# Second half of the row scores issued between the two subtractions on TensorE

## The chip, the cores and the metric

The kernel runs on one core of one Trainium2 chip. The metric is the device time of one execution in microseconds, lower is better. The core has five engines with a program each: TensorE (PE; its weight loads are shown as PEld), VectorE (DVE), ScalarE (ACT), GpSimd (POOL) and SyncE (SP, which here only issues DMAs). They meet through semaphores.

## The reference

32 sequences of 128 tokens, width 128, go through four blocks. In short, with 16 heads of 8:

```
x = block0(x):  x += g * attn(adaLN(x), mask_qk);  x += g * attn(adaLN(x), ctx, mask_kv);  x += g * gelu-MLP(adaLN(x))
x = block1(x):  x += gate * out(mixture of 3 experts over [LN(x), evidence(ctx), anchor])
x = block2(x):  x += attn(adaLN(x), adaLN(ctx))
x = block3(x):  x += attn(adaLN(x));  x += attn(x, ctx);  x += gelu-MLP(adaLN(x))

attn: s = q @ k.T / sqrt(8);  s = where(mask, s, lowest);  a = softmax(s);  out = a @ v
```

Five of these layers are attentions: two over 128 keys (the first of them masked over query and key, with rotary embedding), three over the 77 context tokens (the first masked over keys).

## The kernel before, in words

**Jobs.** An attention layer has 32 jobs, one per sequence; four jobs make a quad, and projections and norms are done per quad. Layers 0 and 1 (jobs 0 to 63) form phase 0, layers 2 to 4 (jobs 64 to 159) phase 1; between the phases stand the first MLP and the mixture of experts, after phase 1 the last MLP. In the text the layers are: masked (128 keys, `l0`), context with key mask (`l0c`, 77 keys), context (`l2`, 77), plain (`l3s`, 128) and last context (`l3c`, 77).

**Two sets of scores.** Each job's scores are made twice. *Row scores* (`rows`, line 645, made in reduced precision into `row_scores`, queries on partitions) serve only to find the maximum of each row; VectorE reads them (`row_max`, line 1215, tile `negmax`). They come in two halves of eight heads, h=0 and h=1, and both halves use the same two PSUM banks: a half can be written only when the maximum of the half before has been taken (the wait on `max_done` in `rows` and, for the masked layer, in `mask_rows`). *Exact scores* (`exact`, line 687, 16 products with keys on partitions into four banks of `scores`) feed the softmax. The row maximum is subtracted on TensorE by a product for each half (`shift`, line 707); then ScalarE takes the exponential of that half (`exponentiate`, line 1723, tile `p`), and `weigh` (line 720) multiplies with the values into `weighed`. `turn_blocks` on VectorE (line 1231, `nat`) takes that out.

**Masks.** In the masked layer mask products of 8 small matmuls each are added: `mask_rows` (closing for h=0, opening for h=1) and `mask_scores` (opening half 0 before the exact scores, closing half 1 after its subtraction).

**The order.** Each engine runs its own loop over slots t; the order inside a slot is written by hand. On TensorE (`attention`, line 757) slot t issued: the opening mask and the row scores of job t+5, half 1; exact scores and both subtractions of job t; `weigh` of job t-1; row scores of job t+6, half 0; then `quad_work`, which is in each quad of four slots a K projection, a transposition (norm or x), a value and output projection, and a Q projection (lines 793 to 817). `exact(t)` waits until both exponentials of job t-1 are done and for the DMAs of the pair (`stack_pair`, line 2116, SP's queue); `scores_read` holds it until a bank of `scores` that `quad_work` used has been read. On VectorE (line 1364) slot t runs: maximum of job t+5 half 1, reciprocal and transposition of older jobs, maximum of job t+6 half 0, norm statistics, rotations, residuals and `turn_blocks` of job t-1. GpSimd spreads the keys for the row scores (`spread_k`, line 1915, tile `kblk_r`), and waits for both halves of job t+5 before it writes those of job t+7.

The names used below: R0 and R1 are the row scores of half 0 and 1 (line 663), E the exact scores (line 700), S0 and S1 the subtractions (line 715), W is `weigh` (line 730).

Of the kernel before, what the change touches and what calls it, by code (L numbers as in the profile page):

```python
# [90 lines left out]
def layer_of(q):  # L91
    return LAYERS[q // NB]
# [92 lines left out]
def build(nc, a, out_x):  # L185
    with ExitStack() as ctx:
# [221 lines left out]
        def folding_at(t, hi):  # L408

            return t - 4 * hi - 5 if 0 <= t - 4 * hi - 5 < FOLDING else None  # L410
# [46 lines left out]
        def turned_in_quads(it):  # L457


            return not it.family or 0 < 4 * PHASES[it.q >= 2 * NB][1] - it.slot <= 5  # L460
# [25 lines left out]
        def row_banks(n, h):  # L486
            return scores[:, 2:4, :] if h == 0 and first_quad(n) else row_scores[:, :, :]

        def row_banks_read(n, h):
            return max_done, 2 * n + h - (1 if first_quad(n) else 0)  # L490
# [44 lines left out]
        def tensor_program(e):  # L535
# [93 lines left out]
            def mask_rows(n, h, opens):  # L629

                if layer_of(n // QUAD).mask == "qk":
                    w.wait_ge(dve_setup, DVE_AT["neg_qk"])
                    w.wait_ge(act_setup, ACT_AT["ident_bf"])
                    if opens:
                        w.wait_ge(*row_banks_read(n, h))
                    for i in range(2):
                        at = slice(TILE * (2 * h + i), TILE * (2 * h + i + 1))
                        for c in range(NG):
                            mm = e.matmul(row_banks(n, h)[TILE * c:TILE * (c + 1), i, :], ident_bf[at, at],
                                          neg_qk[at, c, :].unsqueeze(1).to_broadcast([TILE, NJ, S]), start=opens,  # L640
                                          stop=not opens, skip_group_check=True, tile_position=(TILE * (2 * h + i), TILE * c))
                    if not opens:
                        mm.then_inc(rows_done, 1)
# [113 lines left out]
            def attention(phase, first=-16, last=None):  # L757

                lo, hi = PHASES[phase]
                end = 4 * hi + TAIL if last is None else 4 * lo + last  # L760
                jobs, quads, norm_at = range(4 * lo, 4 * hi), range(lo, hi), NORM_AT[phase]

                def scores_read(t):

                    qi, cl = divmod(t, QUAD)
                    if t in norm_at and not turned_in_quads(norm_at[t]):
                        w.wait_ge(*turned_read(norm_at[t]))
                    if cl == 2 and qi - 2 in quads and qi >= hi:
                        w.wait_ge(wo_read, qi - 1)
                    if cl == 2 and qi + 1 in quads:  # L770
                        w.wait_ge(v_done, qi + 2)

                def quads_read(t):

                    qi, cl = divmod(t, QUAD)
                    if cl == 0 and qi + 2 in quads and qi + 2 != 0:
                        if layer_of(qi + 2).rope:
                            w.wait_ge(rope_half, 4 * (qi + 2) + 4)
                        else:
                            w.wait_ge(k_done, qi + 2 - NB + 1)  # L780
                    if cl == 1 and qi + 3 in quads and layer_of(qi + 3).name == "l3c":
                        w.wait_ge(raw_done, (qi + 3) % NB + 1)
                    if t in norm_at and turned_in_quads(norm_at[t]):
                        w.wait_ge(*turned_read(norm_at[t]))
                    if cl == 2 and qi - 2 in quads and qi < hi:
                        w.wait_ge(wo_read, qi - 1)
                    if cl == 3 and qi + 3 in quads:
                        if layer_of(qi + 3).rope:
                            w.wait_ge(rope_half, 4 * (qi + 3) + 2)
                        else:  # L790
                            w.wait_ge(q_done, qi + 3 - NB + 1)

                def quad_work(t, qi, cl):
                    early = max(min(2 * t + 1, 8 * hi), 8 * lo)
                    if cl == 2 and qi + 1 in quads:
                        w.wait_ge(exp_done, early)
                        project_v(qi + 1)
                    if t in norm_at and not turned_in_quads(norm_at[t]):
                        w.wait_ge(exp_done, early)
                        turn_normed(norm_at[t])  # L800
                    if t == -2 * QUAD:
                        project_k(0)
                    if cl in (0, 3) or t in norm_at or cl == 1 and qi + 3 in quads or cl == 2 and qi - 2 in quads:
                        for back in range(1, QUAD + 1):
                            quads_read(t - back)
                    if cl == 0 and qi + 2 in quads and t != -2 * QUAD:
                        project_k(qi + 2)
                    if cl == 1 and qi + 3 in quads and layer_of(qi + 3).name == "l3c":
                        turn_x(qi + 3)
                    if t in norm_at and turned_in_quads(norm_at[t]):  # L810
                        turn_normed(norm_at[t])
                    if cl == 2 and qi - 2 in quads:
                        if qi >= hi:
                            w.wait_ge(exp_done, early)
                        project_out(qi - 2)
                    if cl == 3 and qi + 3 in quads:
                        project_q(qi + 3)

                for t in range(4 * lo + first, end):
                    qi, cl = divmod(t, QUAD)  # L820
                    masked = t in jobs and layer_of(qi).mask == "qk"
                    if t + 5 in jobs:
                        mask_rows(t + 5, 1, True)
                    if t in (4 * lo, 4 * lo + 1):
                        w.wait_ge(max_done, 8 * lo + 8)
                    if masked:
                        scores_read(t - 1)
                        mask_scores(t, 0)
                    if t + 5 in jobs:
                        rows(t + 5, 1)  # L830
                    scores_read(t - 1)
                    if t in jobs:
                        exact(t)
                        shift(t, 0)
                        shift(t, 1)
                    if masked:
                        mask_scores(t, 1)
                        if cl == 3 and qi + 1 in quads:
                            w.wait_ge(nblk_done, qi + 2)
                    if phase == 1 and t in (4 * lo - 2, 4 * lo - 1):  # L840
                        keep_busy(4, av_bank[:, 0:128])
                    if t == 4 * hi:
                        first_layer(phase, 0, hi, range(2))
                    if t - 1 in jobs:
                        weigh(t - 1)
                    if t + 6 in jobs:
                        rows(t + 6, 0)
                        mask_rows(t + 6, 0, False)
                    if t in (-6, -4, -3):
                        keep_busy(3, scores[:, 0, 0:128])  # L850
                    if not masked and cl == 3 and qi + 1 in quads:
                        turn_max(qi + 1)
                    quad_work(t, qi, cl)
                    if masked and cl == 2 and qi + 1 in quads:
                        turn_max(qi + 1)
                    if phase == 0 and last is None:
                        first_prototypes(t - 4 * hi)
                    if t == -11:
                        modulate(range(2, 9))
                    if t == -8:  # L860
                        gates_and_context()
                    if t == -7:
                        w.wait_ge(act_setup, ACT_AT["l0mod1"])
                        keep_busy(5, scores[:, 0, 0:128])
                    c = first_layer_at(t, hi)
                    if c is not None:
                        first_layer(phase, c, hi, range(0 if c else 2, 4))
                    if second_layer_at(t, hi) is not None:
                        second_layer(phase, second_layer_at(t, hi), hi)
                    if phase == 0 and folding_at(t, hi) is not None:  # L870
                        fold_weights(folding_at(t, hi))
# [1414 lines left out]
```

## Time and profile before

| | us |
|---|---|
| three runs | 1036.22, 1025.52, 1047.08 (median 1036.22) |
| the profiled execution | 1023.18 |
| its span | 1021.4 |
| TensorE busy | 954.0 (93%) |
| VectorE busy | 742.6 (73%) |
| ScalarE busy | 621.7 (61%) |
| GpSimd busy | 616.5 (60%) |

The two attention phases take about 60 to 340 and 580 to 965 us of the span; the stretch between is the first MLP and the experts. A matmul's busy time contains its way through the pipeline, so that slices overlap: the start of the next one tells more than its length. Times in the timeline are us from the start of the span; the bracket at a row's end is the idle time of that engine before it and what ended it.

### The profile page before, as it was taken

Reading aid. Unit: us, or ns where it says so; the run is one execution under the profiler, and the core shown is the slowest. Engines: PE = TensorE matmul, PEld = TensorE weight load, DVE = VectorE, ACT = ScalarE, POOL = GpSimd, SP = SyncE. Lnnn points to the kernel's source line nnn. Section 1 sums busy time; section 2 is a strip of 40 time slices with the busy share of each in tenths; the row PEclk is TensorE's granted clock in tenths of the full one; section 3 lists DMA queues with packets and bytes.
Section 4 is the critical chain, followed back from the end, with each engine's and each line's share of the span. In section 5 each row is a group of like instructions: output and inputs, shape, how many; then the busy total and the mean of one; then the engine's idle time right before and its main releaser. Section 6 shows DMA issues by size and latency. Waiting matters only on the chain.

```text
span 1021.4 us, 31933 instructions
## 1 busy us (share of the span) xinstructions
PE 954.0 (93%) x12961; PEld 651.2 (64%) x12961; DVE 742.6 (73%) x1852; ACT 621.7 (61%) x938; POOL 616.5 (60%) x739
## 2 busy tenths in 40 slices
PE   8789999999989999999999998999999999998998
PEld 5345555566666777666667666666666666666676
DVE  7778888788875443677777879989998867785421
ACT  2144454578766544544455567787677778874762
POOL 6678888677874332122112679977878766686530
PEclk9799999999988999999999999999999999996999
DMA  6622333344442102000000033444343443333011
GB/s 213 218 85 85 130 123 120 112 132 138 135 133 82 43 31 83 26 7 13 7 7 14 7 122 111 129 128 139 117 144 111 142 145 117 127 107 125 2 42 42
DMA packets 101458, 96.88 MB, mean 95 GB/s; under 512 B 11632, under 2 KB 93808, under 8 KB 100928
## 3 DMA queue, kind: packets, MB, share of 16 engines
q1 hardware_dynamic: 101312, 94.84, 28.1%
q8 instruction: 103, 1.69, 0.7%
q14 instruction: 43, 0.35, 0.1%
HBM read 18.77 MB, written 2.15 MB: 20 GB/s over the span
## 4 chain that ended last, share of the span: by engine, by line
PE 67%; POOL 13%; DVE 12%; issue 6%; ACT 1%; DMA 0%; POOLq 0%; SPq 0%; DVEq 0%; ACTq 0%
PE weighed L730 13%; DVE negmax L1220 8%; PE row_scores L663 7%; PE scores L901 6%; PE weighed L753 5%; PE scores L700 4%; PE scores L715 4%; PE scores L618 3%; PE row_scores L901 3%; PE quads L625 3%; POOL kblk_r L1921 3%; PE row_scores L743 2%; PE scores L743 2%; PE weighed L918 2%; PE row_scores L918 2%
## 5 line engine op out<-in xcount | busy, mean ns | idle before, releaser
L1220 DVE TENSOR_REDUCE negmax<-row_scores 128x8 f32<-128x616 f32 (+1 forms) x312 | 299.2, 959 | 102.6 <-PE row_scores L663 74.5
L1732 ACT ACTIVATE p<-scores 128x1024 f32<-128x1024 f32 (+1 forms) x253 | 251.4, 1019 | 111.2 <-PE scores L715 106.7
L1921 POOL TENSOR_TENSOR kblk_r<-work,pack_const 128x308 fp32r<-128x308 f32 (+1 forms) x160 | 134.0, 838 | 75.3 <-PE row_scores L663 69.0
L730 PE MATMUL weighed<-p,v 77*32 77x128 f32 (+1 forms) x5120 | 176.4, 279 | 2.1 <-DVE nat L1236 1.3
L663 PE MATMUL row_scores<-kblk_r,qr 32*128 32x308 f32 (+1 forms) x624 | 141.9, 449 | 26.2 <-DVE negmax L1220 21.3
L730 PEld LDWEIGHTS weighed<-p,v 77*32 77x32 f32 (+1 forms) x5120 | 132.4, 111 | 43.8 <-issue 31.7
L663 PEld LDWEIGHTS row_scores<-kblk_r,qr 32*128 32x128 f32 x624 | 60.8, 188 | 99.9 <-DVE negmax L1220 53.8
L700 PE MATMUL scores<-q_ring,k_ring 32*77 32x128 f32 (+1 forms) x2512 | 117.3, 253 | 3.9 <-DVE hat L1184 2.6
L700 PEld LDWEIGHTS scores<-q_ring,k_ring 32*77 32x77 f32 (+1 forms) x2512 | 95.5, 164 | 8.7 <-DVE hat L1184 4.2
L1964 POOL TENSOR_TENSOR attn<-nat,rden 128x128 f32<-128x128 f32 x160 | 65.0, 406 | 56.5 <-DVE rden L1241 56.2
L715 PE MATMUL scores<-nblk,select 32*77 32x512 bf16 (+1 forms) x628 | 87.5, 390 | 0.4 <-DVE nblk L1227 0.4
L1236 DVE STREAM_TRANSPOSE nat<-weighed 128x256 f32<-128x256 f32 x160 | 70.0, 438 | 9.1 <-PE weighed L730 9.1
L1732 ACT ACTIVATE p<-scores,neg_kb 77x1024 f32<-77x1024 f32 x61 | 65.9, 1107 | 17.3 <-PE scores L715 14.1
L1938 POOL TENSOR_TENSOR xh<-x,mv 128x512 f32<-128x512 f32 x48 | 50.0, 1042 | 25.6 <-ACT rst L1635 25.5
L753 PEld LDWEIGHTS weighed<-layers_w,work 128*128 128x128 f32 x512 | 59.0, 192 | 3.6 <-issue 2.4
L1941 POOL TENSOR_TENSOR xh<-xh,rst 128x512 f32<-128x512 f32 (+1 forms) x56 | 58.3, 1042 | 4.4
L753 PE MATMUL weighed<-layers_w,work 128*128 128x128 f32 x512 | 59.9, 275 | 0.8 <-DVE x L1277 0.8
L2038 POOL TENSOR_TENSOR xh<-x,r_mv 128x512 f32<-128x512 f32 x8 | 8.3, 1044 | 80.5 <-ACT r_rst L1643 79.6
L1906 POOL TENSOR_TENSOR work<-work,qr 128x512 f32<-128x512 f32 x40 | 50.9, 1273 | 0.0
L599 PE MATMUL quads<-work,layers_w 128*128 128x512 f32 x80 | 45.2, 648 | 0.0
L1111 DVE BATCH_NORM_STATS2 bn<-x 128x6 f32<-128x128 f32 x192 | 43.8, 267 | 0.0
L1248 DVE STREAM_TRANSPOSE attnT<-attn 128x128 f32<-128x128 f32 x160 | 40.9, 256 | 2.8 <-POOL attn L1964 2.8
(334 smaller groups left out, 1914.4 us busy)
## 6 DMA issues: line engine op xcount, KB each, us to landing
q_ring<-work SPq DMA_DIRECT2D x160, 128.0 KB, 2.1
q_ring<-qr SPq DMA_DIRECT2D x160, 128.0 KB, 2.1
k_ring<-k_high SPq DMA_DIRECT2D x64, 128.0 KB, 2.1
k_ring<-work SPq DMA_DIRECT2D x64, 128.0 KB, 2.1
k_ring<-k_high SPq DMA_DIRECT2D x96, 77.0 KB, 2.0
k_ring<-work SPq DMA_DIRECT2D x96, 77.0 KB, 2.0
shared<-gates_hbm SPq DMA_DIRECT2D x24, 256.0 KB, 3.4
shared<-in_ctx_tok SPq DMA_DIRECT2D x15, 154.0 KB
```

The source lines that it names most:

```text
L663: mm = e.matmul(row_banks(n, h)[:, i, 0:cols], qr[q % 3][at, s * S:(s + 1) * S], kblk_r[n % 2][at, 0:cols], start=layer.mask is None or ma ...
L700: mm = e.matmul(score_banks(n, g // 2)[0:nk, g % 2, j * S:(j + 1) * S], keys_of(m, nk)[at, j, half * nk:(half + 1) * nk].bitcast(F32R), q_ ...
L715: mm = e.matmul(score_banks(n, h)[0:nk, i, :], select[at, s, 0:nk], nblk[q % 2][at, :], start=False, stop=not masked_after, skip_group_che ...
L730: mm = e.matmul(av_bank[TILE * j:TILE * j + TILE, i2 * S:(i2 + 1) * S], v[0:nk, at:at + TILE], p[n % 2][0:nk, g * NJ + j, :], start=i1 == ...
L753: mm = e.matmul(mlp_out_bank[:, s * D:(s + 1) * D], mlp_h[c % 2][k][:, s * S:(s + 1) * S], W[weight][:, k * D:(k + 1) * D], start=(k == 0) ...
L901: mm = e.matmul(bank, weight, src, start=(part == 0), stop=(part == 1))
L1220: e.tensor_reduce(negmax[q % 2][:, 2 * h:2 * h + 2, s * NJ:(s + 1) * NJ], row_banks(n, h)[:, :, 0:NJ * nk].rearrange("p g (j k) -> p g j k ...
L1236: e.transpose(nat[n % 2][:, :, :].rearrange("p c (i s) -> p (c i) s", i=NG), av_bank[:, weighed_cols].rearrange("p (i b s) -> p b i s", i= ...
L1732: e.activation(p[n % 2][0:nk, 8 * h:8 * h + 8, :], score_banks(n, h)[0:nk].rearrange("p g (j q) -> p (g j) q", j=NJ), ACT.Exp, bias=hide, ...
L1921: e.tensor_tensor(kblk_r[n % 2][:, 0:NJ * nk].rearrange("p (j k) -> p j k", j=NJ), k_of[q % 3][:, s * nk:(s + 1) * nk].unsqueeze(1).to_bro ...
L1941: e.tensor_tensor(hat_x, hat_x, rst[f][i][0:it.n, :].unsqueeze(2).to_broadcast([it.n, QUAD, D]), ALU.mult).then_inc(ln_xhat, 1)
L1964: e.tensor_tensor(attn[n % 2][:, :].rearrange("p (k d) -> p k d", d=HD), nat[n % 2][:, :, :].rearrange("p i (k c) -> p (i k) c", c=16)[:, ...
```

## The change

Inside TensorE's slot, R1 (with its opening mask product) moves from ahead of the exact scores to between S0 and S1. The wait of `scores_read`, which stood after R1 (in the masked layer before it as well), now stands first. Nothing is added or removed, and the programs of VectorE, ScalarE, GpSimd and SyncE are the same.

```diff
                 for t in range(4 * lo + first, end):
                     qi, cl = divmod(t, QUAD)
                     masked = t in jobs and layer_of(qi).mask == "qk"
-                    if t + 5 in jobs:
-                        mask_rows(t + 5, 1, True)
                     if t in (4 * lo, 4 * lo + 1):
                         w.wait_ge(max_done, 8 * lo + 8)
+                    scores_read(t - 1)
                     if masked:
-                        scores_read(t - 1)
                         mask_scores(t, 0)
-                    if t + 5 in jobs:
-                        rows(t + 5, 1)
-                    scores_read(t - 1)
                     if t in jobs:
                         exact(t)
                         shift(t, 0)
+                    if t + 5 in jobs:
+                        mask_rows(t + 5, 1, True)
+                        rows(t + 5, 1)
+                    if t in jobs:
                         shift(t, 1)
                     if masked:
                         mask_scores(t, 1)
```

## Rows read from the trace of the kernel before

**Rows 1.** Waits of TensorE, whole span: who waited for whom, total us, times, longest.

```profile
PE row_scores L663 <- DVE negmax L1220: 21.3, 55, 1.4
PE row_scores L639 <- DVE negmax L1220: 11.6, 23, 1.6
PE row_scores L658 <- DVE negmax L1220: 5.7, 15, 0.9
...
PE scores L700 <- DVE hat L1184: 2.6, 7, 0.7
```

**Rows 2.** Windows: length, then busy us (instructions) of PE PEld DVE ACT POOL, clock, DMA.

```profile
700.32:818.67 118.35, 108.26 (x1801) 73.49 (x1801) 104.20 (x203) 84.05 (x117) 92.87 (x110) 1.00 0.39 131
841.07:914.41 73.34, 70.27 (x1317) 48.35 (x1313) 56.57 (x134) 60.16 (x85) 51.86 (x73) 1.00 0.38 123
```

**Rows 3.** Timeline of TensorE, two slots of the last layer: start, us, what [idle before].

```profile
871.61 0.41 PE L663 MATMUL row_scores<-kblk_r,qr 32*128 32x308 f32 x2
871.94 0.79 PE L610 MATMUL quads<-ctxT,layers_w 128*128 128x308 f32 x2
872.91 0.41 PE L663 MATMUL row_scores<-kblk_r,qr 32*128 32x308 f32 x2 [0.18 <-DVE negmax L1220]
...
873.25 0.38 PE L715 MATMUL scores<-nblk,select 32*77 32x512 bf16 x2
...
873.73 1.08 PE L730 MATMUL weighed<-p,v 77*32 77x128 f32 x32
874.75 0.41 PE L663 MATMUL row_scores<-kblk_r,qr 32*128 32x308 f32 x2
...
876.05 0.41 PE L663 MATMUL row_scores<-kblk_r,qr 32*128 32x308 f32 x2 [0.32 <-DVE negmax L1220]
```

**Rows 4.** Timeline of VectorE, the second of those slots.

```profile
875.20 0.80 DVE L1220 TENSOR_REDUCE negmax<-row_scores 128x8 f32<-128x616 f32 x1 [0.71 <-PE row_scores L663]
...
876.51 0.80 DVE L1220 TENSOR_REDUCE negmax<-row_scores 128x8 f32<-128x616 f32 x1 [0.15 <-PE row_scores L663]
```

**Rows 5.** Timeline of ScalarE, the first of those slots.

```profile
873.67 1.93 ACT L1732 ACTIVATE p<-scores 77x1024 f32<-77x1024 f32 x2 [0.39 <-PE scores L715]
```

**Rows 6.** Timeline of TensorE, a slot whose exact products come late.

```profile
898.17 0.50 PE L700 MATMUL scores<-q_ring,k_ring 32*77 32x128 f32 x16 [0.29 <-DVE hat L1184]
...
898.81 1.08 PE L730 MATMUL weighed<-p,v 77*32 77x128 f32 x32
```

**Rows 7.** Timeline of TensorE, two slots of the unmasked 128-key layer.

```profile
755.38 0.50 PE L663 MATMUL row_scores<-kblk_r,qr 32*128 32x512 f32 x2 [0.73 <-DVE negmax L1220]
...
759.95 0.50 PE L663 MATMUL row_scores<-kblk_r,qr 32*128 32x512 f32 x2
...
760.69 0.39 PE L715 MATMUL scores<-nblk,select 32*128 32x512 bf16 x2
...
762.01 0.50 PE L663 MATMUL row_scores<-kblk_r,qr 32*128 32x512 f32 x2
```

**Rows 8.** Timeline of VectorE, the same two slots.

```profile
756.18 1.21 DVE L1220 TENSOR_REDUCE negmax<-row_scores 128x8 f32<-128x1024 f32 x1
...
760.49 1.22 DVE L1220 TENSOR_REDUCE negmax<-row_scores 128x8 f32<-128x1024 f32 x1
```

**Rows 9.** Timeline of TensorE, a slot of the masked layer.

```profile
92.02 0.41 PE L639 MATMUL row_scores<-neg_qk,ident_bf 32*32 32x512 bf16 x8 [0.30 <-DVE negmax L1220]
92.05 0.41 PE L681 MATMUL scores<-neg_kq,ident_bf 32*32 32x512 bf16 x8
92.39 0.50 PE L663 MATMUL row_scores<-kblk_r,qr 32*128 32x512 f32 x2
...
93.12 0.39 PE L715 MATMUL scores<-nblk,select 32*128 32x512 bf16 x2
93.44 0.41 PE L681 MATMUL scores<-neg_kq,ident_bf 32*32 32x512 bf16 x8
```

**Rows 10.** Timeline of VectorE, the same slot.

```profile
93.47 1.18 DVE L1220 TENSOR_REDUCE negmax<-row_scores 128x8 f32<-128x1024 f32 x1
```

## The prediction

> **What bounds the kernel now.** I read the slices of the span first, then the waits of TensorE, then the windows of the stretches in which a quad's pattern repeats, and last the timelines of single slots there. In the attention phases TensorE is the engine that is busy nearly all the time, and of what it waits for, the maxima of the row scores are the main part: 21.3 + 11.6 + 5.7 = 38.6 us of idle time [rows 1]. That is all the change can win, since it moves only the point at which R1 waits for the maximum of R0. Whether it wins depends on who else is full. The windows split the layers in two kinds. In the plain 128-key layer VectorE is busy 104.20 of 118.35 us, 88%; in the last context layer 56.57 of 73.34 us, 77%, with TensorE at 70.27 us, 96% [rows 2]. So in the narrow (77-key) layers TensorE sets the pace, and in the wide ones the reader has to look for VectorE.
>
> The timelines say it more exactly. Row scores and maxima form one loop through two PSUM banks: R0, its maximum, R1, its maximum, the next R0. In a narrow slot R0 starts at 874.75, its maximum at 875.20 and takes 0.80, and R1 starts at 876.05, TensorE idle 0.32 before it [rows 3, 4]. From R0 to R1 is thus never under 1.30, whatever the quad work between them. From R1 to the next R0 it is 874.75 - 872.91 = 1.84, although the loop needs only 1.30 there too [rows 3]. The old order gives the first gap too little TensorE work and the second more than it needs; the new order takes E and S0 out of the second and puts them into the first.
>
> **The change, part by part.** No instruction is added or removed and no DMA moves in the program. All stretches outside the attention phases keep their order, so I charge them nothing. SP's ring transfers wait for E, which gets earlier or stays; I charge nothing, and if that cover fails it shows as E waiting for a DMA.
>
> *Narrow slots, gain.* E starts behind the quad work without R1's wait, S0 starts 873.25 - 872.91 = 0.34 behind it, and R1 then comes where its maximum is already there: 0.34 is more than the 0.18 or 0.32 that it waited [rows 3]. The idle time goes and TensorE's work is the same. A slot with a K projection wins 0.18 and one with a transposition 0.32; the slots with value and output projections and with Q projections have no such idle time and win nothing. I counted 19 and 18 of them in the narrow stretches where GpSimd is not late as well: 19 x 0.18 + 18 x 0.32 = 9.2 us. The cover is thin in two places. VectorE: the second maximum ends at 876.51 + 0.80 = 877.31, which is 2.56 behind its slot's R0 at 874.75; TensorE alone needs more than that, so VectorE is not late there [rows 3, 4]. ScalarE: both exponentials run from 873.67 for 1.93, to 875.60 [rows 5]. E of the next job could not start before R1 at 876.05; it would now start 0.18 + 0.32 earlier, at 875.55, and S0 of this slot, and so the exponentials, come 0.18 earlier too and end at 875.42. They still end first, by 0.13. If not, the narrow gain ends there: bounds 0 and 9.2, and I take 9.2 since these rows decide for that side.
>
> *Slots with late exact scores, loss.* Where a transposition used a bank of `scores`, E waits for VectorE to read it. In the old order R1 had been issued during that wait; now it stands behind. E to W was 898.81 - 898.17 = 0.64 with R1 out of the way [rows 6], and is 873.73 - 872.91 = 0.82 with it [rows 3]. So 0.18 is lost in each, 7 times by the row for the norm [rows 1] and twice for the values' copy: 1.6 us. If R1's maximum then also delays the next R0, it is at most R1's own shift of about 0.35, so 3.2 us.
>
> *Plain layer.* In a slot with a transposition R1 waits 0.73 [rows 7], but here VectorE takes the maximum of R1 only at 756.18, after other work, although R1 was there by 755.38 + 0.50 = 755.88; it ends at 757.39 [rows 7, 8] and releases the next R0. VectorE's order is the same, so this slot keeps its length; only TensorE's wait changes place. In a slot with value and output projections VectorE takes R1's maximum at 760.49, just as R1 (759.95 + 0.50) arrives [rows 7, 8]. Now R1 starts behind E and S0, about 0.45 later: an estimate between the 0.34 to S0 in a narrow slot [rows 3] and the 760.69 - 759.95 = 0.74 to S1 here. Its maximum runs 760.94 to 762.16 and the next R0 starts near 762.26 instead of 762.01: 0.25 lost, in six such slots, 1.5 us. Bounds: 0, and 32 slots at 0.25, 8 us.
>
> *Masked layer.* The opening mask product of R1 used to be issued together with that of the exact scores, 0.03 apart (92.02, 92.05), and one gap of 92.39 - 92.05 = 0.34 led on to the row scores [rows 9]. Now it stands alone between S0 and R1. I price the two new changes of product shape by the nearest rows: 93.44 - 93.12 = 0.32 from a subtraction to a mask product, 0.34 from there to R1 [rows 9], less the 0.03 and about 0.09 because E no longer shares the array with R1: 0.54 a slot. Against that stands the idle time before the mask product, 0.30 [rows 9]. In the 12 slots with rotations (K and Q projections) 0.24 is lost net, 2.9 us. Four slots with value and output projections have no idle time to give: 4 x 0.54 = 2.2 us. The transposition slots have more idle time than 0.54, but VectorE sets their end, so they stay. VectorE's second maximum starts at 93.47, after a rotation and a transposition, not when R1 arrives [rows 10], so even a free mask product wins nothing: bounds 0 and 32 x 0.54 = 17 us, taken 5.1.
>
> The page TensorEngine Tiling (Array Packing) of the Trainium skill, section Key Properties, says that a change of tiling mode, not only of the tile, drains TensorE. No row shows a mask product on one half of the array behind a subtraction on the other half. By that rule both new changes cost their full gap, and the sum is the one below; without it the mask product would start beside S0, as the two mask products 0.03 apart do, and the sum would be some 5 us lower.
>
> *GpSimd.* It waits for R1 before it spreads later keys, so it starts up to 0.35 later in slots without idle time. The keys are needed over a slot later; charged nothing.
>
> **Sum.** -9.2 + 1.6 + 1.5 + 5.1 = -1.0 us. The profiled execution took 1023.18, so it would become 1022.2. That execution is the shortest of four; the median of the three runs is 13 us higher. I set the sum against the mean of the four, (1023.18 + 1025.52 + 1036.22 + 1047.08) / 4 = 1033.0, and predict **1032**. About 2% is what a measurement of this kernel can tell from no change, since its own runs lie 2% apart.
>
> **The rivals.**
>
> *All of TensorE's waits go.* If VectorE could use its gaps, the whole 38.6 us would go: 994. For it: the loop is then balanced. Against: 88% busy in the plain layer, and second maxima that start late for VectorE's own reasons [rows 2, 8, 10]. Chance 0.08.
>
> *R1 becomes the last link of the wide slots.* Between S0 and S1 it is in series with the exact scores: whatever delays E delays R1, its maximum, and the next R0. It decides wherever R1 would now arrive after VectorE is free for it. If that holds in all 64 wide slots, the price is 32 x 0.25 + 32 x 0.54 = 25 us, and the late slots 1.6 more: 1033 + 27 = 1060. For it: the slot at 759.95, where nothing is spare. Against: the other plain slots and the rotations leave VectorE late by more than the shift. Chance 0.14. The rule of the tiling page is its masked half.
>
> *ScalarE closes the narrow gain.* E needs both exponentials of the job before. With 1.93 us for the pair and 0.13 spare [rows 5], one cast in front of them is enough to make E wait. Then -9.2 falls away: 1033 + 8.2 = 1041. Chance 0.15.
>
> **How the numbers follow.** The forecast has 0.63. Its own costs reach from about -10 (nothing lost) to +8, and single executions lie up to 14 us from their mean. That gives 1016 to 1049, which holds the ScalarE case and the milder part of the slower one, and leaves out the faster one: about 0.2 outside. Faster by over 2%: the first rival, 0.08. Slower by over 2%: the worse two thirds of the second, 0.09, and 0.02 for an unlucky measurement: 0.11. Within 2%: 0.81.
>
> **What would show it.** Narrow slots: the idle time before R1 gone, R0 to R0 at 2.96 with a K projection, where it was 874.75 - 871.61 = 3.14, and 0.32 shorter with a transposition. Plain layer: TensorE's waits for the maxima still there, now behind S0, its slots with transpositions unchanged and some with value projections 0.25 longer. Masked layer: mask product some 0.3 behind S0. I am wrong if the narrow slots keep their length, with ScalarE's exponentials in front of E, or if plain slots without idle time grow as well, or if the wide layers get shorter.

## The result: slower, and the profile after

The changed kernel takes 1083.53 us (median of 4 runs, 1076.37 to 1105.70) against 1035.6 us; the ratio is 1.0474, 95% interval 1.0354 to 1.0594. The profiled execution took 1085.71 us, 62.5 us more than the profiled one before. The ratios, here and below, leave out runs that are over 1.5% above the fastest of their kernel, so that they are not always those of the medians.

The slices of the span come first, here as in every reading. This is the line of TensorE's granted clock on the page of the kernel before, in tenths of full speed for 40 equal slices, and below it the engines' busy line and the same clock line on the page after.

```profile
PEclk9799999999988999999999999999999999996999
```

```profile
PE 1029.0 (95%) x12961; PEld 672.2 (62%) x12961; DVE 746.1 (69%) x1852; ACT 622.6 (57%) x938; POOL 616.7 (57%) x739
...
PEclk9655569999999799999999999699999999998999
```

The same number of matmuls keeps TensorE busy for 75 us more, and the slices from the second to the sixth stand at 5 and 6. The granted clock has two levels here, 2.4 GHz (1.0) and 1.2 GHz (0.5). In the trace after, it is at 1.2 GHz from 39.9 to 155.9 us, in one piece. In the trace before, it was at 2.4 GHz from 57.2 to 292.7 us. Here are windows of the kernel after (columns as in [rows 2]): two in the first jobs of the masked layer, one in its later jobs, and one in the last context layer, which answers to the second row there (the same jobs). The first stretch before stands behind them for comparison.

```profile
60.00:100.00 40.00, 39.43 (x404) 19.41 (x403) 18.31 (x36) 10.33 (x14) 18.95 (x20) 0.50 0.16 54
100.00:150.00 50.00, 49.43 (x513) 24.44 (x509) 23.57 (x49) 15.07 (x20) 21.82 (x26) 0.50 0.25 86
156.00:260.00 104.00, 103.64 (x1831) 59.54 (x1823) 81.05 (x173) 52.91 (x74) 75.15 (x87) 1.00 0.31 103
...
906.52:979.40 72.88, 70.83 (x1314) 47.67 (x1313) 56.45 (x133) 59.92 (x86) 51.91 (x72) 1.00 0.39 125
```

```profile
60.00:100.00 40.00, 36.55 (x729) 21.21 (x726) 33.63 (x71) 19.36 (x27) 29.09 (x34) 1.00 0.30 102
```

TensorE is about 99% busy or more in the three masked windows of the kernel after, yet the first 40 us hold 404 matmuls where before they held 729. A busy share doesn't tell at which clock the engine is busy.

TensorE's waits did shrink as the change intends. Columns as in [rows 1], kernel after:

```profile
PE row_scores L663 <- DVE negmax L1219: 9.5, 34, 1.4
PE scores L700 <- DVE hat L1183: 7.5, 9, 1.6
...
PE scores L700 <- DMA q_ring<-qr: 3.5, 4, 1.3
...
PE scores L715 <- DVE nblk L1226: 2.7, 9, 0.5
PE scores L618 <- ACT p L1731: 2.0, 8, 0.3
PE row_scores L639 <- DVE negmax L1219: 1.7, 1, 1.7
```

For the maxima 9.5 + 1.7 = 11.2 us are left of 38.6. What they gave up was not won.

Where the time went is seen best from W to W, since each job has one. The table gives, against the profiled execution before, how much longer each stretch takes (us; from the first `weighed` product of the one job to that of the other), for the kernel after and for five of the kernels below. "To job 0" runs from the span's start; 31-64 contains the context layer with key mask, the first MLP and the experts, 64-75 the start of the context layer. The low stretches are those at 1.2 GHz between 39 and 200 us and between 590 and 700 us (start, length). Shorter ones stand elsewhere in every profile: the kernel before has 17.1 us of them in 31-64 and 17.1 in 128-158, the kernel after 13.7 and 10.2, and 3.4 in 75-96.

| kernel | to job 0 | 0-10 masked | 10-31 masked | 31-64 | 64-75 | 75-96 context | 96-128 plain | 128-158 last context | low stretches |
|---|---|---|---|---|---|---|---|---|---|
| after | 6.6 | 42.0 | 3.8 | 0.3 | 8.4 | 2.7 | 2.6 | -3.9 | 39.9 + 116.1; 678.2 + 20.5 |
| steady | 0.1 | 0.0 | 4.0 | 5.0 | 0.4 | 2.2 | 2.6 | -4.0 | 42.1 + 10.2 |
| fed_after | 2.9 | 41.5 | 3.8 | -1.2 | 0.1 | 1.5 | 2.6 | -3.8 | 52.1 + 99.0 |
| masks_paired | 4.1 | 3.7 | 0.5 | -1.5 | 21.5 | 2.5 | 2.7 | -4.0 | 40.8 + 30.7; 607.4 + 58.0 |
| narrow_steady | 2.9 | 6.9 | 0.0 | -1.4 | 0.0 | -0.8 | -0.3 | -4.2 | 41.6 + 37.5 |
| fed_narrow | -2.8 | -0.1 | -0.1 | -3.3 | 4.4 | -1.3 | -0.2 | -4.1 | 627.0 + 10.2 |

In the kernel after the first ten masked jobs carry 42.0 of the 62.5 us. This is the timeline of TensorE there: one slot at the low clock, the slot in which the clock rose, and a slot at the high clock (it answers to [rows 9]).

```profile
126.66 1.12 PE L700 MATMUL scores<-q_ring,k_ring 32*128 32x128 f32 x16
127.58 0.65 PE L715 MATMUL scores<-nblk,select 32*128 32x512 bf16 x2
128.16 0.62 PE L639 MATMUL row_scores<-neg_qk,ident_bf 32*32 32x512 bf16 x8
128.72 0.80 PE L663 MATMUL row_scores<-kblk_r,qr 32*128 32x512 f32 x2
...
136.16 1.12 PE L700 MATMUL scores<-q_ring,k_ring 32*128 32x128 f32 x16
...
151.62 2.08 PE L618 MATMUL scores<-layers_w,work 128*128 128x128 f32 x8
153.49 1.92 PE L625 MATMUL quads<-layers_w,attnT 128*128 128x128 f32 x8
...
155.99 0.67 PE L700 MATMUL scores<-q_ring,k_ring 32*128 32x128 f32 x16
...
177.96 0.67 PE L700 MATMUL scores<-q_ring,k_ring 32*128 32x128 f32 x16
178.46 0.39 PE L715 MATMUL scores<-nblk,select 32*128 32x512 bf16 x2
178.78 0.41 PE L639 MATMUL row_scores<-neg_qk,ident_bf 32*32 32x512 bf16 x8
179.12 0.50 PE L663 MATMUL row_scores<-kblk_r,qr 32*128 32x512 f32 x2
...
183.29 0.67 PE L700 MATMUL scores<-q_ring,k_ring 32*128 32x128 f32 x16
```

The low slot with a K projection is 136.16 - 126.66 = 9.50 long, the one with a Q projection at the high clock 183.29 - 177.96 = 5.33, and no row of the low one waits for anything. The clock rose at 155.9, at the end of the first slot with a value projection and an output projection one behind the other (eight products of the whole array; each is two instructions in the trace, x8 and x8 in the rows). The first ten jobs have no output projection, since it follows two quads later.

### The profile page after: what moved, and what is told of

The parts are those of the page before. It is cut to its first block, busy times and chain, and to the rows that moved or that the text cites. A ratio compares the mean times of both kernels' runs of the same rounds, so it can differ in the third digit from the quotient of the medians.

```text
span 1083.9 us, 31936 instructions
## 1 busy us (share of the span) xinstructions
PE 1029.0 (95%) x12961; PEld 672.2 (62%) x12961; DVE 746.1 (69%) x1852; ACT 622.6 (57%) x938; POOL 616.7 (57%) x739
## 4 chain that ended last, share of the span: by engine, by line
PE 71%; DVE 10%; issue 7%; POOL 7%; ACT 2%; SPq 1%; DMA 1%; POOLq 0%; ACTq 0%; DVEq 0%
PE weighed L730 10%; PE row_scores L663 6%; PE scores L900 6%; PE scores L700 6%; PE weighed L753 5%; PE scores L715 5%; DVE negmax L1219 5%; PE scores L618 4%; PE row_scores L900 3%; PE quads L625 3%; PE scores L681 2%; PE quads L610 2%; PE row_scores L639 2%; PE quads L599 2%; PE row_scores L743 2%
## 5 line engine op out<-in xcount | busy, mean ns | idle before, releaser
L730 PE MATMUL weighed<-p,v 77*32 77x128 f32 (+1 forms) x5120 | 188.3, 292 | 1.9 <-DVE nat L1235 1.3
L730 PEld LDWEIGHTS weighed<-p,v 77*32 77x32 f32 (+1 forms) x5120 | 140.5, 116 | 55.0 <-issue 34.0
L663 PE MATMUL row_scores<-kblk_r,qr 32*128 32x308 f32 (+1 forms) x624 | 146.1, 463 | 13.7 <-DVE negmax L1219 9.5
L700 PEld LDWEIGHTS scores<-q_ring,k_ring 32*77 32x77 f32 (+1 forms) x2512 | 75.2, 173 | 73.0 <-issue 28.4
L715 PE MATMUL scores<-nblk,select 32*77 32x512 bf16 (+1 forms) x628 | 114.6, 409 | 2.7 <-DVE nblk L1226 2.7
L700 PE MATMUL scores<-q_ring,k_ring 32*77 32x128 f32 (+1 forms) x2512 | 98.5, 272 | 14.5 <-DVE hat L1183 7.5
L663 PEld LDWEIGHTS row_scores<-kblk_r,qr 32*128 32x128 f32 x624 | 64.2, 199 | 55.4 <-issue 31.2
L599 PE MATMUL quads<-work,layers_w 128*128 128x512 f32 x80 | 49.2, 699 | 0.0
L715 PEld LDWEIGHTS scores<-nblk,select 32*77 32x77 bf16 (+1 forms) x628 | 35.5, 110 | 15.6 <-issue 9.6
L1719 ACT COPY v<-scores 77x512 f32<-77x512 f32 (+1 forms) x40 | 23.3, 583 | 36.7 <-PE scores L618 35.8
```

What stands on the lines that cost most here:

```text
L599: mm = e.matmul(quad_bank[:, at], W[layer.wq], xn[q % 3][:, at], start=True, stop=True)
L663: mm = e.matmul(row_banks(n, h)[:, i, 0:cols], qr[q % 3][at, s * S:(s + 1) * S], kblk_r[n % 2][at, 0:cols], start=layer.mask is None or ma ...
L700: mm = e.matmul(score_banks(n, g // 2)[0:nk, g % 2, j * S:(j + 1) * S], keys_of(m, nk)[at, j, half * nk:(half + 1) * nk].bitcast(F32R), q_ ...
L715: mm = e.matmul(score_banks(n, h)[0:nk, i, :], select[at, s, 0:nk], nblk[q % 2][at, :], start=False, stop=not masked_after, skip_group_che ...
L730: mm = e.matmul(av_bank[TILE * j:TILE * j + TILE, i2 * S:(i2 + 1) * S], v[0:nk, at:at + TILE], p[n % 2][0:nk, g * NJ + j, :], start=i1 == ...
```

## The experiments

The names in the table are those of runs in this section. All edits are to TensorE's program; `late` chooses for each slot between the new order and the old one.

**Where it is lost.** masked_only: new order in the masked layer alone.

```diff
+ late = t < 4 * NB      # new order where late, old order elsewhere
```

> The new order in the slots of phase 0's first layer (and the slots ahead of it) alone, the old one from job 32 on. Theory A (the clock): in the new order the masked slots, once entered at the granted clock 0.5, stay there until the first slot with value and output projections, so nearly all of the loss is here: ratio to before 1.04 to 1.06, granted clock 0.92 to 0.94, one stretch of 0.5 of about 100 us. Theory B (the loss is spread over all attention slots as a wait of R1): ratio 1.01 to 1.02.

1077.69 us (1076.33 to 1081.18), ratio 1.0456 (1.0393 to 1.0519), low from 42.0 to 154.7 us. Nearly the whole loss.

unmasked_only: the other 128 jobs alone.

```diff
+ late = t >= 4 * NB
```

> The old order in the masked layer's slots, the new one from job 32 on. Theory A: the clock is as before (0.96 to 0.98) and the rest is a small matter, ratio 0.99 to 1.01, with one open point: the 20 us at 0.5 in the first context slots of phase 1, which would add 9 us if it comes back. Theory B: ratio 1.02 to 1.03.

1050.67 us (1044.50 to 1059.76), ratio 1.0196 (1.0115 to 1.0277). The masked layer is at 2.4 GHz from 52.8 us on. A second low stretch stands at the start of the context layer, 605.7 to 663.8 us. TensorE's timeline where it ends, with the same two projections for the first time in that phase:

```profile
661.01 1.99 PE L618 MATMUL scores<-layers_w,shared 128*77 128x128 f32 x8
662.79 1.53 PE L625 MATMUL quads<-layers_w,attnT 128*128 128x128 f32 x8
```

So both phases begin badly, the second by a varying amount: with the new order there, six profiles (one of them, filled, with added products) show 0 to 58 us at 1.2 GHz between 590 and 700 us; with the old order, eight show 0 to 10.2.

**Is a late start the cause?** warm: the changed kernel, with 40 whole-array products ahead of the first jobs.

```diff
+ if t in (-2, -1):
+     keep_busy(20, av_bank[:, 0:128])
```

> The changed kernel with 40 extra 128x128x128 fp32 products on TensorE in the two slots ahead of the first job (about 9 us at the low clock, 4.5 at the high one, partly in idle time). Theory A, in the form that the order only fails to lift a low clock but holds a high one: the masked layer runs at 1.0, its slots at 4.9 to 5.3 and 6.4, ratio 1.00 to 1.02. If the order cannot hold the high clock either without whole-array products, it falls back within some slots: ratio 1.03 to 1.05. Theory B: unchanged, 1.045 or more.

1085.75 us (1084.59 to 1091.48), ratio 1.0540 (1.0473 to 1.0607). Windows of this kernel:

```profile
59.20:66.10 6.90, 5.55 (x66) 3.28 (x65) 2.71 (x5) 1.23 (x2) 0.76 (x1) 0.99 0.00 0
66.10:165.00 98.90, 97.20 (x947) 48.64 (x947) 45.41 (x92) 27.21 (x38) 46.42 (x50) 0.50 0.19 65
```

The clock was high behind the products, and fell in the slot of job 0, with TensorE 98% busy from there on. It is not a missing push at the start.

**What brings it back.** filled: the changed kernel, with eight whole-array products (16 instructions) where later quads have the output projection, which has four.

```diff
  exact(n):
+     if n in (3, 7, 67, 71):
+         keep_busy(8, scores[:, 3, 0:128])
```

> The changed kernel, with eight more whole-array products (128 x 128, results never used) right behind the waits of the exact scores in jobs 3 and 7 of the masked layer and jobs 3 and 7 of the context layer: beside the value projection of the slot before they stand where the output projection stands in all later quads. Nothing else is moved. Theory (the slots without an output projection are too thin in the new order for TensorE to be granted 2.4 GHz, and the whole-array products of value and output projection together bring it): the 1.2 GHz stretch of the masked layer, 116 us in the changed kernel, ends near 75 to 90 us instead of 156, the dip of 20 us at the context layer goes or is shorter, and 25 to 45 us come back: 1038 to 1060, ratio 1.00 to 1.025. Rival (the low clock after the start has another cause, such as the time since the last busy stretch): the stretch still ends near 156, ratio 1.045 or more, since the products add about 3 us.

1054.14 us (1053.40 to 1057.15), ratio 1.0226 (1.0151 to 1.0301). As expected: about half of the loss comes back. TensorE's timeline:

```profile
76.41 2.08 PE L618 MATMUL scores<-layers_w,work 128*128 128x128 f32 x8
...
79.72 3.78 PE L565 MATMUL scores<-pack_const 128*128 128x128 f32 x16
```

The low stretch ends at 83.7 instead of 155.9 us, in the very slot with the added products, and the new order held 2.4 GHz from there. That they, and not the time since the start, brought the clock is shown by this pair.

**Which part of the change costs the clock.** masks_paired: R1 in its new place, its opening mask product beside that of the exact scores as before (diff against the changed kernel).

```diff
+ if t + 5 in jobs: mask_rows(t + 5, 1, True)
  ...
  exact(t)
  shift(t, 0)
  if t + 5 in jobs:
-     mask_rows(t + 5, 1, True)
      rows(t + 5, 1)
```

> The changed kernel, but the opening mask product of R1 goes back beside the opening mask product of the exact scores (the old place); only R1 itself stays between the subtractions. If the separate mask product is what thins out the array's work in a cold slot: clock as before, ratio 0.99 to 1.01. If it is R1's place, no longer beside the exact scores: the cold stretch stays, ratio 1.04 to 1.05.

1050.10 us (1031.96 to 1056.36; too scattered for a ratio). Windows of this kernel, the two low stretches:

```profile
40.80:71.50 30.70, 27.23 (x269) 13.14 (x269) 15.31 (x26) 8.53 (x13) 17.81 (x19) 0.50 0.35 118
607.40:665.40 58.00, 56.66 (x619) 36.49 (x620) 33.80 (x103) 28.94 (x47) 37.90 (x49) 0.50 0.28 89
```

In the masked layer the clock rose at 71.5, with no output projection issued. The context layer's start stayed low.

paired_late: the same, with the old order in jobs 64 to 75.

```diff
+ late = not 4 * lo <= t < 4 * lo + 12 or phase == 0
```

> As the kernel of the run with paired masks (the opening mask product of R1 stays beside that of the exact scores, ahead of E; R1 itself between S0 and S1), but the first twelve jobs of the second phase wholly in the old order. Theory (the lone mask product keeps the masked layer at 1.2 GHz, and R1 taken from beside E does it at the start of the context layer; the rest is slot cost of under 1%): the masked layer's low stretch ends where runs with the old order there end it, between 50 and 95 us of the span, no low stretch at 605 us, and the time is that of the kernel before plus 0 to 8 us: ratio 1.000 to 1.010. Rival (R1's move alone costs the clock in the masked layer as well): low until 155 us, 1.03 or more.

1042.97 us (1031.50 to 1060.49), ratio 1.0141 (1.0082 to 1.0200): more than expected. The masked layer is low until 79.9, as expected, and the stretch at 605 us is gone, but a short one (649.9, 6.8 us) and one in the context layer with key mask (254.0, 13.7 us, 31-64 is 5.3 us longer by W to W) remain. So the lone mask product is the part that holds the masked layer at 1.2 GHz, and R1's own move can cost the clock at the start of the context layer. Why a lone product does so is not shown, and why short stretches of 13.7 us come and go elsewhere stays open; nearly all profiles have some, the one before at 303.0 and 931.0.

**What the order costs at the high clock.** steady: the first twelve jobs of each phase in the old order, all others in the new.

```diff
+ late = t >= 4 * lo + 12
```

> New order only from the thirteenth job of each attention phase on (jobs 12 to 63 and 76 to 159); the first twelve jobs of both phases in the old order. Theory (the loss is the clock in the first slots of a phase, which have no output projection yet): the 1.2 GHz stretches are those of the kernel before, and what is left is the slots' cost at the high clock, by the slot lengths of the two traces 5 quads x 1.05 in the masked layer, 8 x 0.63 in the plain one, about -1.5 in the last context layer and what the context layers add: 4 to 9 us, ratio 1.003 to 1.012. Rival (the new order lowers the clock or lengthens the slots wherever it stands): with 136 of 160 jobs in the new order at least 1.03.

1042.78 us (1029.32 to 1082.94), ratio 1.0047 (0.9987 to 1.0107), as expected. By that ratio 136 of 160 jobs in the new order cost under 1.1%. But four of the ten runs came out above 1060 us, at a mean granted clock of 0.913 to 0.932 (the other six 0.956 to 0.970); of the 29 runs of the kernel before taken with them none passed 1055. These were not followed up: in some runs the new order may cost the clock behind the first twelve jobs as well.

plain_only: the plain layer alone.

```diff
+ late = t in jobs and layer_of(qi).name == "l3s"
```

> New order only in the unmasked 128-key layer (jobs 96 to 127). By the slot lengths of the two traces at the same clock, 16.93 against 16.30 us a quad, 8 quads: 5 us more, ratio 1.003 to 1.007. My prediction had 1.5 us for it, with bounds 0 and 8. Rival (the clock falls in that layer when it alone stands in the new order): a new 1.2 GHz stretch between 700 and 830 us and 1.015 or more.

1039.26 us (1025.92 to 1053.55), ratio 1.0021 (0.9957 to 1.0086), below what was expected and not resolved. By W to W the layer takes 2.7 us more. The next one, in the old order, takes 1.6 less, all of it behind job 149, where 13.7 us are at 1.2 GHz and 17.1 in the kernel before. The 5 us came from single quads, and the layer's edges don't follow them. This run's masked layer is wholly in the old order, and yet low until 92.2 us, with the profiled execution at 1038.8. In narrow_steady, with the old order there as well, it is low until 79.1. How long the old order takes to reach 2.4 GHz thus varies from run to run, which may be part of the spread of the kernel before.

**Versions that may beat both.** narrow_steady: the new order only in 77-key slots behind a K projection or a transposition in `quads`.

```diff
+ late = (t in jobs and not masked and layer_of(qi).nk == SK and t >= 4 * lo + 12 and cl in (1, 2)
+         and not (t - 1 in norm_at and not turned_in_quads(norm_at[t - 1])))
```

> New order only where the two traces show a gain: in the 77-key layers, from the thirteenth job of a phase on, in the slots behind a K projection and behind a transposition whose result does not stand in a bank of the exact scores; everywhere else the old order. Theory: 0.24 and 0.27 us a slot, in some 30 slots: 7 to 9 us less, ratio 0.991 to 0.994; with the context layers gaining less than the last one, down to 4 us, 0.996. Rival (a slot in the old order behind one in the new gives the gain back, since R0 is then as late as ever): no difference, 0.998 to 1.002. Second rival: the thinner slots lose the clock in the narrow layers too: above 1.005.

1032.37 us (1023.26 to 1048.82), ratio 0.9949 (0.9897 to 1.0000). By W to W -1.4 - 0.8 - 4.2 = -6.4 us in the narrow layers; about 2.0 of them come behind job 149, where the short low stretches are 3.4 us shorter. The gain is there, at the edge of what can be measured.

fed_narrow: the same, with 17 whole-array products in TensorE's waits of 2.85 us (for `kblk_r`) and 1.42 us (for `negmax`) ahead of the masked layer, in front of its second low stretch.

```diff
  rows(n, h):
+     if h == 0 and n in (4, 5):
+         keep_busy(12 if n == 4 else 5, scores[:, 0, 0:128])
```

> The kernel with the new order only in the gaining narrow slots, and 17 whole-array products more (128 x 128, results never used) where TensorE waits 2.85 and 1.42 us before the masked layer: 12 ahead of the row scores of job 4, 5 ahead of those of job 5. In seven traces the clock was at 1.2 GHz from about 41 us on, behind these waits, and ended it between 52 and 92 us where the masked layer has the old order. Theory (whole-array products in the idle time keep or bring 2.4 GHz early): no low stretch, or one that ends before 57 us; the late lifts go, the runs come closer together, and the median falls by 5 to 12 us below that without the products: ratio 0.982 to 0.992. Rival (the clock after the waits is not settled by 4 us of products): low stretches as before, ratio 0.993 to 1.000.

1019.40 us (1010.07 to 1036.71), ratio **0.9831** (0.9749 to 0.9912): faster than both kernels. TensorE's timeline:

```profile
38.38 2.94 PE L565 MATMUL scores<-pack_const 128*128 128x128 f32 x24
41.30 0.50 PE L665 MATMUL row_scores<-kblk_r,qr 32*128 32x512 f32 x2
```

The products fill the wait, and the clock stays high from 33.1 us to 295.9. The runs did not come closer together.

fed_before and fed_after: the same 17 products in the kernel before, and in the changed one.

```diff
+ late = False           # fed_before
+ late = True            # fed_after
```

> The kernel before with these 17 products and nothing else. It splits the last run's gain of 17 us. By the run with the narrow slots alone, 0.9949, the products are worth 0.983 / 0.995 = 0.988: ratio 0.984 to 0.992, no low stretch between 40 and 100 us. Rival (the products do all of it, and the narrow slots win nothing): 0.980 to 0.984.

1024.76 us (1019.85 to 1054.96), ratio 0.9915 (0.9870 to 0.9960). Of the 1.7% about half are the products', by these two ratios; the intervals overlap, so the share of the narrow slots is not measured closely.

> The changed kernel with the same 17 whole-array products in TensorE's waits before the masked layer. With them the old order there ran at 2.4 GHz from 33 us of the span on. Theory (the new order's slots without an output projection neither bring nor hold 2.4 GHz): the clock falls to 1.2 GHz within the first masked jobs, as it did at 66 us in the run with products ahead of the first job, and stays there until the first slot with value and output projection: ratio 1.03 to 1.05. Rival (the new order only can't raise the clock, but holds it once it is high): no low stretch between 40 and 160 us, and with the context layer's short dip 1.00 to 1.015.

1073.07 us (1070.61 to 1081.79), ratio 1.0393 (1.0317 to 1.0469). TensorE's timeline around the fall, and a window behind it:

```profile
50.47 0.39 PE L717 MATMUL scores<-nblk,select 32*128 32x512 bf16 x2 [1.16 <-DVE nblk L1235]
50.78 0.41 PE L639 MATMUL row_scores<-neg_qk,ident_bf 32*32 32x512 bf16 x8
...
53.03 0.79 PE L665 MATMUL row_scores<-kblk_r,qr 32*128 32x512 f32 x2 [0.84 <-DVE negmax L1228]
```

```profile
100.00:150.00 50.00, 49.43 (x489) 25.06 (x482) 23.88 (x51) 12.68 (x19) 20.39 (x23) 0.50 0.22 76
```

High from 35.0 to 52.1 us, then down in the slot of job 0, and up again at 151.1 in the first slot with an output projection. The rival is refuted: the new order's early slots don't hold 2.4 GHz, while in fed_narrow the old order held it through the same jobs. Whether the two waits shown, 1.16 and 0.84 (0.56 and 0.49 in fed_narrow), had a part in the fall was not told apart; the 99 us after it, 98% busy, are not theirs.

## Why the prediction was wrong

**The step that failed** is the masked layer's, and before it the first sentence of the parts, by which all costs were durations at the clock of their rows. The lone mask product was priced at 0.54 a slot, with 32 x 0.54 = 17 us as the bound. All these rows come from a stretch granted at 1.0, and no term says what happens if the clock isn't granted. In the first ten jobs it wasn't, and a slot took 9.50 us there instead of about 5.3. The clock's part: of the first ten jobs 42.0 less 10 x 3.8 / 21 = 1.8 for the order at the high clock (an estimate from jobs 10 to 31), so 40.2; 6.6 ahead of job 0; and at the context layer's start 8.4 - 0.1 = 8.3, by fed_after, which has no low stretch there. Together 55 of the 62.5 us; the 6.6 and 8.3 are taken as clock as a whole. That the mask product is the part of the change that costs it in the masked layer is shown by masks_paired and paired_late; that the clock is the price, by filled and steady. I read the slices first, but not the clock's line among them: it showed that the kernel before, too, came up from 1.2 GHz only at the start of this layer.

**The sum at the high clock** was off as well. fed_after, leaving out jobs 0 to 10, has 3.8 - 1.2 + 0.1 + 1.5 + 2.6 - 3.8 = 3.0 us. Two of these terms contain the clock: in 31-64 and 128-158 this kernel has 13.7 and 10.2 us at 1.2 GHz, the kernel before 17.1 and 17.1. That this weighs is seen where the old order stands in the last layer: masked_only has +1.5 us there with 20.5 low, plain_only -1.6 with 13.7. Up to the jobs ahead of these stretches (53 and 149) fed_after has +0.1 and -0.9 instead of -1.2 and -3.8. With these, and 1.8 for jobs 0 to 10, the sum is 1.8 + 3.8 + 0.1 + 0.1 + 1.5 + 2.6 - 0.9 = 9.0 us (an estimate, without the last jobs of the two layers), where I had -1.0. Together with the 55 it is 64 for 62.5 measured.

*Masked layer.* 3.8 us in 21 jobs, which makes 5.8 in 32; predicted 5.1. From W to W a quad's slots change by +0.61 (value and output projection), +0.18, +0.37 and -0.11; I had 0.54, 0.24, 0.24 and 0. The gaps came as priced: S0 to mask product 178.78 - 178.46 = 0.32, mask product to R1 0.34. With that the rule of the Trainium skill, TensorEngine Tiling (Array Packing), Key Properties, that a change of tiling mode drains TensorE, agrees with the trace: the mask product did not start beside S0.

*Narrow slots.* TensorE's timeline in the slots of [rows 3], kernel after, with the slot ahead of them, behind a Q projection; the same slot before stands below:

```profile
935.61 0.50 PE L700 MATMUL scores<-q_ring,k_ring 32*77 32x128 f32 x16
...
936.11 0.41 PE L663 MATMUL row_scores<-kblk_r,qr 32*128 32x308 f32 x2
...
936.66 1.08 PE L730 MATMUL weighed<-p,v 77*32 77x128 f32 x32
937.67 0.41 PE L663 MATMUL row_scores<-kblk_r,qr 32*128 32x308 f32 x2
938.01 0.79 PE L610 MATMUL quads<-ctxT,layers_w 128*128 128x308 f32 x2
938.72 0.50 PE L700 MATMUL scores<-q_ring,k_ring 32*77 32x128 f32 x16
939.05 0.38 PE L715 MATMUL scores<-nblk,select 32*77 32x512 bf16 x2
939.06 0.35 PE L663 MATMUL row_scores<-kblk_r,qr 32*128 32x308 f32 x2
...
940.57 0.41 PE L663 MATMUL row_scores<-kblk_r,qr 32*128 32x308 f32 x2
...
943.44 0.40 PE L663 MATMUL row_scores<-kblk_r,qr 32*128 32x308 f32 x2
```

```profile
869.76 0.41 PE L663 MATMUL row_scores<-kblk_r,qr 32*128 32x308 f32 x2
869.76 0.67 PE L700 MATMUL scores<-q_ring,k_ring 32*77 32x128 f32 x16
...
870.60 1.08 PE L730 MATMUL weighed<-p,v 77*32 77x128 f32 x32
```

R0 to R0 is 940.57 - 937.67 = 2.90 with the K projection (2.96 forecast) and 943.44 - 940.57 = 2.87 with the transposition (3.13 in the trace before, 0.32 less forecast), and R1 now starts with S0. Both waits are gone and no E waits for an exponential here (in the whole span three do, 1.5 us), so the ScalarE rival is refuted; eight value projections wait for them, 2.0 us (one before, 0.3). But the narrow layers together gave nothing: 0.1 + 0.1 + 1.5 - 0.9 = 0.8 us lost (fed_after, up to jobs 53 and 149), where 9.2 - 1.6 = 7.6 were to be won. Missing in the sum were, first, the slots behind a Q projection, which I had at nothing. R1 ran beside E there, and E to W took 870.60 - 869.76 = 0.84; now R1 comes behind S0 and it takes 936.66 - 935.61 = 1.05, so 0.21 is lost in each, with no wait. Second, E waits for the DMA of `q_ring`, 3.5 us in all, and nowhere in the trace before: SP's cover, charged nothing, failed in the way the prediction named. Third, the wait for `hat` grew from 2.6 to 7.5 us, where I had counted only R1 standing behind it; four such slots of the last layer are about 0.3 longer, not 0.18. And S0 waits for `nblk`, 2.7 us in all, against 0.4 before, most of it in the plain layer.

*Plain layer.* 2.6 us, with 1.5 predicted; the same kernel's TensorE there:

```profile
824.66 0.67 PE L700 MATMUL scores<-q_ring,k_ring 32*128 32x128 f32 x16
...
825.17 0.44 PE L663 MATMUL row_scores<-kblk_r,qr 32*128 32x512 f32 x2
...
827.03 0.50 PE L663 MATMUL row_scores<-kblk_r,qr 32*128 32x512 f32 x2 [0.17 <-DVE negmax L1219]
...
828.53 0.67 PE L700 MATMUL scores<-q_ring,k_ring 32*128 32x128 f32 x16
829.45 0.39 PE L715 MATMUL scores<-nblk,select 32*128 32x512 bf16 x2 [0.24 <-DVE nblk L1226]
```

R1 starts 0.51 behind E, and the next R0 waits for its maximum: the mechanism forecast for slots with value and output projections. The last row is the wait for `nblk`.

*The rivals.* That all waits go was half right, 38.6 became 11.2, and worthless. The slower one, R1 as the last link of all wide slots, had the right sign and place, but its 25 us were to come from loops and gaps; at the high clock the wide layers lost 5.8 + 2.6 = 8.4.

## What to carry to other kernels

Before pricing a reorder on TensorE, read the granted clock stretch by stretch, above all where a phase starts: work that runs side by side and is pulled apart costs its own gaps, and may cost the clock of everything around it, which in the masked layer was some eight times as much (40.2 + 6.6 us against 5.8). A TensorE that is 99% busy may be so because it is slow; count matmuls per stretch beside the share. And where a phase opens with waits, a few whole-array products in them can be worth more than the order of the work behind them.

## What was not expected of the hardware

TensorE stayed at 1.2 GHz for 116 us while 95% busy or more (99% from 60 to 150 us), and rose in the first slot with a value and an output projection one behind the other, eight whole-array products, in four profiles of the new order (at 155.9, 154.7, 165.1 and 151.1 us), or earlier where eight were added (83.7). The Trainium skill, TensorE: Matmul & The Clock Gate, section What's actually happening, puts the price of the ramp up from 1.2 GHz at under 1% of a typical kernel's span; here the time at 1.2 GHz cost about 5% (55 of 1023 us). And the same order comes to 2.4 GHz at different times: with the old one in the first masked jobs, between 52.4 and 92.2 us in five profiles without added products.
